# Key scores of a product-key memory laid out key by key instead of head by head, on one Trainium2 core

## The chip, the core and the metric

The kernel runs on one core of a Trainium2 chip. Its engines are TensorE (PE: matmul; PEld: weight load), VectorE (DVE), ScalarE (ACT), GpSimd (POOL) and the DMA queues, here all issued by SyncE (SP). The metric is device time in microseconds for one execution of the whole program. An SBUF tensor has 128 partitions; "elements" below are the fp32 values of one partition, and a step is the distance between neighbours in the order in which an instruction goes through them.

## The reference, cut to what matters

The program is a two-layer decoder over 8192 tokens of width 128: attention, cross attention and a memory layer, then attention, cross attention and a mixture of experts. The change lies in the memory layer, a product-key memory with 8 heads and 2 x 32 keys for each head:

```
q = (xn @ w_q.T).reshape(b, n, 2, h, kd).transpose(2, 0, 1, 3, 4)
sim = jnp.einsum('pbnhd,hkpd->pbnhk', q, keys)
s, i = jax.lax.top_k(sim, k)
all_scores = (sx[..., :, None] + sy[..., None, :]).reshape(b, n, h, k * k)
scores, pk = jax.lax.top_k(all_scores, k)
o = jnp.einsum('bnd,bnhkd->bnhk', inputs, w_down)
o = jax.nn.gelu(o, approximate=False) * jax.nn.softmax(scores, axis=-1)
return jnp.einsum('bnhk,bnhkd->bnd', o, w_up)
```

For each token and head: 32 scores on each of two sides, the 8 best of each side, the 8 best of their 64 sums, and a softmax over those 8 that weighs 8 of 1024 experts.

## The kernel before, in words

A tile is 128 tokens, one in each partition; there are 64 tiles. The memory stage runs all of them through a software pipeline: `staggered` takes, for each engine, a list of (lag, step), and in each round an engine runs its steps in the written order, a step of lag l on the tile l rounds back. Two rounds are one turn of the hardware loop. Each engine works through its list strictly in order; semaphores tie the engines together.

What happens to a tile, with the lines of the profile:

- ACT `normed` L857, then PE `key_scores` L1246: one matmul of the tile against `Mk`, 512 columns = 2 sides x 8 heads x 32 keys, into PSUM bank 0. `Mk` is written once at the start of the program (ACT, L696).
- DVE `top_keys` L1773: 16 MAX8 of 32 scores each, one per side and head, give the 8 best (`V8`). DVE `less_best` L1782: all 512 scores less the best of their side and head, into `DIFF`. DVE `best_less` L1791: the same for the 8 best.
- ACT `key_exps` L864, L865: exp of both, into `EX`; the keys' exps go between other terms there, at a step of 5 x 8 floats. ACT `best_one_hot` L878: one-hot of the best key.
- POOL `candidates` L616, L619: products of the best exps. POOL `terms` L630 to L641: four terms for each key and head, written into `EX` and `hots`. POOL `second_one_hot` L646.
- DVE `top_pairs` L1800 (8 MAX8), `pair_floors` L1807, `pair_sums` L1812, `pair_shares` L1817: the 8th best pair of each head, and one over the sum.
- ACT `above_floor` L897: 8 instructions, one per head, write into PSUM (`psABOVE`) where a term is above the floor. DVE `chosen` L1824: the minimum of that and the term, into `sides`. ACT `scaled_one_hots` L887: 8 instructions, one per head, write the one-hots times the share into `sides`.
- DVE `turn_sides` L1832, L1833: transposes in blocks of 32. PE `spread_heads` L1263: 256 small matmuls make the weights of the 1024 experts, in PSUM banks 0 and 1. DVE `turn_back` L1839 transposes them, PE `turn_weights` L1271 turns them again.
- PE `hidden` L1251 and ACT `hidden` L903 (gelu): the token against all 1024 experts. DVE `gated` L1845: product of both. PE `mixed` L1277: times the experts' outputs. DVE `add_memory` L1849 adds it to the token, `stats_with_memory` L1854 takes its statistics.

PSUM bank 0 holds the scores of one tile and then half of the expert weights of an earlier one. So `spread_heads` of a tile waits until `less_best` of the tile four rounds later has read its scores:

```
pe.wait_ge(d_ready, T.ahead(4, 0, NT))
```

The order on each engine is written out by hand:

```
staggered(nc, pe, NT, [(6, mixed), (0, key_scores), (4, hidden), (5, turn_weights), (4, spread_heads)])
staggered(nc, dve, NT, [(2, top_pairs), (0, top_keys), (2, pair_floors), (2, pair_sums), (7, stats_with_memory), (0, less_best), (3, chosen), (5, gated),
                        (3, turn_sides), (4, turn_back), (5, add_memory), (2, pair_shares), (0, best_less)])
staggered(nc, act, NT, [(0, normed), (2, exps_before_gelu), (5, hidden), (2, exps_after_gelu), (2, best_one_hot), (3, above_floor),
                        (3, scaled_one_hots)])
staggered(nc, pool, NT, [(0, candidates), (1, second_one_hot), (0, terms)])
```

The exps come before the gelu in every second round and after it in the others, so that ACT loads one table set in a round.

Before the change the scores of a tile lie as side, head, key, with the key innermost. `DIFF` and `hots` lie in the same order; `EX` and `sides` lie key by key, with the head innermost.

Of the kernel before, what the change touches and what calls it, by code (L numbers as in the profile page):

```python
# [7 lines left out]
P = 128  # L8
# [11 lines left out]
NKEY = 32  # L20
BLOCK = 32
PH = 8
# [13 lines left out]
ALU = mybir.AluOpType  # L36
ACT = mybir.ActivationFunctionType
# [39 lines left out]
def need(eng, sem, value):  # L77

    if isinstance(value, int) and value <= 0:
        return  # L80
    eng.wait_ge(sem, value)
# [26 lines left out]
def build(nc, x, ctxT, ctx, mask, consts, rows, cols, wq0, wk0, wv0, wo0, xWq, xWk, xWvT, xWeT, wqk, keysT, key_inT,  # L108
# [3 lines left out]
    with ExitStack() as es:  # L112
        def sb(name, shape, dt=F32):
            return es.enter_context(nc.sbuf_tensor(name, shape, dt))

        def sem(name):
            return es.enter_context(nc.semaphore(name))
# [13 lines left out]
        Mk = sb("Mk", [P, 2 * PH * NKEY])  # L131
# [20 lines left out]
        def C(name):  # L152
            a, n = CONST[name]
            return cst[:, a:a + n]
# [24 lines left out]
        top = [0]  # L179

        def carve(n):
            a = top[0]
            top[0] += n
            assert top[0] <= WORK, top[0]
            return work[:, a:a + n]
# [53 lines left out]
        NS = PH * NKEY  # L239
        BEST = 2 * PH * TOPK  # L240
# [4 lines left out]
        DIFF = carve(2 * (BEST + 2 * NS)).rearrange("p (u n) -> p u n", u=2)  # L245
        EX = carve(2 * (BEST + 5 * NS)).rearrange("p (u n) -> p u n", u=2)
        V8 = carve(2 * BEST).rearrange("p (u n k) -> p u n k", u=2, k=TOPK)
# [2 lines left out]
        Z = carve(2 * PH).rearrange("p (u h) -> p u h", u=2)  # L250
        FLOOR = carve(2 * PH).rearrange("p (u h) -> p u h", u=2)
        RZ = carve(2 * PH).rearrange("p (u h) -> p u h", u=2)
        hots = carve(4 * 2 * NS).rearrange("p (r s h k) -> p s r h k", r=4, s=2, h=PH)
        IN2 = [hots[:, :, 2 + u] for u in range(2)]
        KI = carve(NEXP)
        sides = carve(8 * NS)
        XY = sides.rearrange("p (k n h) -> p n h k", n=8, h=PH)
        XT = carve(2 * NEXP).rearrange("p (u k t) -> p u k t", u=2, k=NKEY)
        YT = carve(2 * NEXP).rearrange("p (u k t) -> p u k t", u=2, k=NKEY)
        WT = carve(NEXP)  # L260
# [5 lines left out]
            return DIFF[:, u, 0:BEST].rearrange("p (s h k) -> p s h k", s=2, h=PH)  # L266

        def keys_diff(u):
            return DIFF[:, u, BEST:].rearrange("p (s h k) -> p s h k", s=2, h=PH)

        def by_key(u):
            return EX[:, u, BEST:].rearrange("p (k n h) -> p k n h", n=5, h=PH)

        def keys_of(u):
            return by_key(u)[:, :, 0:2].rearrange("p k s h -> p s h k")

        def best_of(u):
            return EX[:, u, 0:BEST].rearrange("p (s h k) -> p s h k", s=2, h=PH)

        def terms_of(u):  # L280
            return by_key(u)[:, :, 1:5]

        WIDE_Y, REST, DEEP_X = 1, 2, 3
        FAR = 2.0 ** 100
        NEXT_BELOW = 1.0 - 2.0 ** -24
        chosen_terms = XY[:, 2:6].rearrange("p n h k -> p k (n h)")
        one_hot_sides = sides.rearrange("p (k a r h) -> p a r h k", a=4, r=2, h=PH)[:, 0:4:3]
        x_side, y_side = [sides.rearrange("p (k a n) -> p k a n", k=NKEY, a=4)[:, :, a:4:2] for a in range(2)]

        def one_hots_of(u):  # L290
            return hots[:, :, u:4:2]
# [46 lines left out]
        ps = es.enter_context(nc.psum_tensor("ps", [P, 8, 512], F32))  # L338

        def bank(b, a, n=P):  # L340
            return ps[:, b, a:a + n]
# [14 lines left out]
        def group_bank(b, n=P):  # L356
# [7 lines left out]
        psTurn, psRoute = group_bank(6), group_bank(6, MOE)  # L364

        psW = ps[:, 0:2, :].rearrange("p q (k t) -> p q k t", k=NKEY)
        psABOVE = ps[:, 2:4, :].rearrange("p q (k n h) -> p (q k) n h", n=4, h=PH)
        psG = ps[:, 4:6, :].rearrange("p b (c d) -> p (b c) d", d=P)
        psH = ps[:, 6:8, :].rearrange("p b (c d) -> p (b c) d", d=P)
        psM = bank(4, 0)  # L370
        psSim = ps[:, 0, :]
# [24 lines left out]
        ones_ready, sums_done, quantised, folds_done, folds_ready, bound_ready = (  # L396
            sem("ones_ready"), sem("sums_done"), sem("quantised"), sem("folds_done"), sem("folds_ready"), sem("bound_ready"))
# [27 lines left out]
        xb_ready, sim_done, v8_ready, d_ready, ex_ready = (  # L425
            sem("xb_ready"), sem("sim_done"), sem("v8_ready"), sem("d_ready"), sem("ex_ready"))
# [98 lines left out]
        def _(pool):  # L525
# [5 lines left out]
            for u in range(2):  # L531
                ins = pool.tensor_copy(VB[:, u, :], C("vones_pairs"))
# [12 lines left out]
            for n, part in enumerate((bias_parts[:, 0], bias_parts[:, 1], bias_rest[:, 1])):  # L545
                to = bias_rest[:, 2] if n == 2 else bias_rest[:, 0] if n == 0 else bias_b[:, :]
                ins = pool.tensor_tensor(to, part, part_rows[:, n:n + 1].to_broadcast([P, P]), ALU.mult)
# [75 lines left out]
            def terms(T):  # L623

                u = T.u
                x, y = keys_of(u)[:, 0], keys_of(u)[:, 1]
                second = best_of(u)[:, :, :, 1:2].to_broadcast([P, 2, PH, NKEY])
                rest, deep, wide = [terms_of(u)[:, :, n].rearrange("p k h -> p h k") for n in (REST, DEEP_X, WIDE_Y)]
                need(pool, scaled_ready, T.before(2))
                pool.tensor_tensor(IN2[u], keys_of(u), second, ALU.subtract).then_inc(less_second, 1)  # L630
                pool.tensor_tensor(wide, y, second[:, 0], ALU.mult)
                pool.wait_ge(less_second, T.now())
                pool.sem_inc(rank_seen, 1)
                pool.tensor_scalar(IN2[u], IN2[u], 0.0, None, ALU.is_ge).then_inc(in2_ready, 1)
                pool.wait_ge(in2_ready, T.now())
                pool.sem_inc(rank_seen, 1)
                pool.tensor_scalar(rest, IN2[u][:, 0], -1.0, 1.0, ALU.mult, ALU.add).then_inc(far_ready, 1)
                pool.wait_ge(far_ready, T.now())
                pool.tensor_tensor(rest, rest, x, ALU.mult).then_inc(rest_ready, 1)
                pool.wait_ge(rest_ready, T.now())  # L640
                pool.tensor_tensor(deep, rest, second[:, 1], ALU.mult).then_inc(terms_ready, 1)  # L641
# [45 lines left out]
        def _(act):  # L687
# [5 lines left out]
            act.activation(small[:, A1, :], bank(0, 0), ACT.Copy)  # L693
            act.activation(small[:, A2, :], bank(0, P), ACT.Copy)
            act.activation(sc[:, 30:31], bank(5, 0, 1), ACT.Copy)
            act.activation(Mk[:, :], ps[:, 1, :], ACT.Copy).then_inc(folds_ready, 1)  # L696

            def deviations(n, width=NT):
                act.wait_ge(var_ready, n)
# [160 lines left out]
            def key_exps(T):  # L860
                need(act, xy_ready, T.before(2))
                act.wait_ge(d_ready, T.now())
                act.wait_ge(best_less_ready, T.now())
                act.activation(EX[:, T.u, 0:BEST], DIFF[:, T.u, 0:BEST], ACT.Exp)  # L864
                act.activation(keys_of(T.u), keys_diff(T.u), ACT.Exp).then_inc(ex_ready, 1)  # L865

            def exps_before_gelu(T):
                if T.u == 1:
                    key_exps(T)
# [5 lines left out]
            def best_one_hot(T):  # L875
                act.wait_ge(d_ready, T.now())
                need(act, scaled_ready, T.before(2))
                act.activation(hots[:, :, T.u], keys_diff(T.u), ACT.Relu, scale=FAR, bias=1.0).then_inc(top_ready, 1)  # L878

            def scaled_one_hots(T):  # L880

                u = T.u
                act.wait_ge(hot_ready, T.now())
                act.wait_ge(rz_ready, T.now())
                need(act, sides_ready, T.before(1))
                for h in range(PH):
                    ins = act.activation(one_hot_sides[:, :, :, h, :], one_hots_of(u)[:, :, :, h, :], ACT.Copy, scale=RZ[:, u, h:h + 1])  # L887
                ins.then_inc(scaled_ready, 1)

            def above_floor(T):  # L890
# [28 lines left out]
            for e in range(0, MOE, 2):  # L919
                ins = act.activation(d_up[:, e:e + 2].rearrange("p e c d -> p (e c d)"),  # L920
                                     down_w[:, e:e + 2].rearrange("p e c d -> p (e c d)"), ACT.Copy)
# [494 lines left out]
        def _(dve):  # L1416
# [345 lines left out]
            dve.sem_inc(phase, 1)  # L1762


            sim = psSim.rearrange("p (n k) -> p n k", k=NKEY)

            def top_keys(T):

                need(dve, best_less_ready, T.before(2))
                dve.wait_ge(sim_done, T.now())  # L1770
                dve.sem_inc(sim_seen, 1)
                for n in range(2 * PH):
                    ins = dve.max(V8[:, T.u, n, :], sim[:, n, :])  # L1773
                ins.then_inc(v8_ready, 1)

            def less_best(T):

                u = T.u
                top = V8[:, u].rearrange("p (s h) k -> p s h k", s=2)[:, :, :, 0:1]
                dve.wait_ge(v8_ready, T.now())  # L1780
                need(dve, top_ready, T.before(2))
                dve.tensor_tensor(keys_diff(u), sim.rearrange("p (s h) k -> p s h k", s=2), top.to_broadcast([P, 2, PH, NKEY]),  # L1782
                                  ALU.subtract).then_inc(d_ready, 1)

            def best_less(T):
# [33 lines left out]
            def chosen(T):  # L1819

                u = T.u
                dve.wait_ge(share_ready, T.now())
                need(dve, sides_ready, T.before(1))
                dve.tensor_tensor(chosen_terms, psABOVE.rearrange("p k n h -> p k (n h)"), terms_of(u).rearrange("p k n h -> p k (n h)"), ALU.min)\  # L1824
                    .then_inc(xy_ready, 1)

            def turn_sides(T):
# [296 lines left out]
```

## Time and profile before

| | |
|---|---|
| time, median of 3 runs | 2624.07 us (2623.74 to 2628.8) |
| the profiled execution's own time | 2623.28 us |
| its span, first to last instruction | 2621.5 us |
| mean granted TensorE clock | 0.945 of full |
| memory stage, first to last L1263 | 611.6 to 1300.7 us |
| busy over the whole span | PE 89%, DVE 78%, ACT 76%, POOL 35% |

The span is one execution as the hardware profiler saw it. "Busy" is the time in which an engine had an instruction under way; instructions of one engine overlap a little at their ends, so the sum of durations is larger than the time they fill. What an instruction costs the next one is better read from the distance between starts. A wait is the idle time of an engine before an instruction, put down to what released it.

### The profile page before, as it was taken

How to read it: one execution, taken by the hardware profiler on the slowest of the kernel's cores; microseconds unless marked ns; L12 is line 12 of the kernel's file. 1: busy time of each engine (PE TensorE's matmuls, PEld its weight loads, DVE VectorE, ACT ScalarE, POOL GpSimd, SP SyncE). 2: the span in 40 equal slices, each digit the busy share in tenths (PEclk: the TensorE clock that was granted, in tenths of full speed). 3: DMA queues.
4: the chain of work that ended last, by engine and by line, in shares of the span. 5: the costliest groups of instructions: out<-in, count | busy, mean ns of one | idle time of the engine just before them, and what ended most of it. 6: DMA issues, size and time to landing. Idle time of an engine off the chain costs nothing.

```text
span 2621.5 us, 95503 instructions
## 1 busy us (share of the span) xinstructions
PE 2336.3 (89%) x34892; PEld 1856.8 (71%) x34892; DVE 2032.4 (78%) x5455; ACT 1987.0 (76%) x3656; POOL 926.1 (35%) x1203
## 2 busy tenths in 40 slices
PE   2999943966888899988889999899899999999999
PEld 1676733645888888888857767566688788888887
DVE  6788889667799999999667777688766777777776
ACT  1888852778799999999667777788567777777776
POOL 1555510337677777777433333233100000000000
PEclk9999975987799999999899999899799999999999
DMA  5000000000000000000020000111111111111111
GB/s 183 1 0 0 0 17 0 1 0 3 1 0 0 0 0 0 0 0 0 3 66 0 0 0 0 35 44 43 30 43 45 49 57 52 57 51 54 52 57 45
DMA packets 56808, 64.82 MB, mean 25 GB/s; under 512 B 7696, under 2 KB 35088, under 8 KB 56592
## 3 DMA queue, kind: packets, MB, share of 16 engines
q1 hardware_dynamic: 56720, 63.65, 8.0%
q8 instruction: 54, 0.88, 0.1%
q14 instruction: 34, 0.28, 0.0%
HBM read 59.17 MB, written 4.46 MB: 24 GB/s over the span
## 4 chain that ended last, share of the span: by engine, by line
PE 78%; DVE 9%; issue 6%; ACT 4%; SPq 1%; POOL 1%; DVEq 1%; ACTq 0%; POOLq 0%; DMA 0%
PE ps L1263 9%; PE ps L1121 5%; PE ps L1078 5%; PE ps L1106 5%; PE ps L1277 5%; PE ps L1351 4%; PE ps L1373 4%; PE ps L1375 4%; PE ps L1374 4%; PE ps L1353 4%; PE ps L1352 4%; PE ps L1134 3%; PE ps L1093 3%; PE ps L1165 2%; PE ps L1029 2%
## 5 line engine op out<-in xcount | busy, mean ns | idle before, releaser
L562 POOL TENSOR_TENSOR work<-work,consts_sb 128x1024 f32<-128x1024 f32 x128 | 245.9, 1921 | 389.5 <-ACT work L729 346.8
L1263 PE MATMUL ps<-work 32*32 32x32 f32 x16384 | 249.4, 225 | 74.4 <-DVE work L1782 60.2
L1263 PEld LDWEIGHTS ps<-work 32*32 32x32 f32 x16384 | 242.1, 145 | 88.8 <-issue 88.8
L1991 DVE TENSOR_TENSOR h_low<-consts_sb,h_up 128x1024 fp32r<-128x1024 f32 x128 | 156.7, 1224 | 116.3 <-ACT h_up L967 116.3
L1589 DVE TENSOR_REDUCE work<-ps 128x8 f32<-128x512 f32 x256 | 169.8, 686 | 84.8 <-PE ps L1078 79.0
L897 ACT ACTIVATE ps<-work 128x128 f32<-128x128 f32 x512 | 216.6, 478 | 4.0 <-POOL work L641 3.3
L1351 PE MATMUL ps<-a_low,w_up 128*128 128x512 f32 x512 | 205.9, 402 | 0.0
L1373 PE MATMUL ps<-h_low,d_up 128*128 128x512 f32 x512 | 199.9, 390 | 2.2 <-DVE h_low L1991 2.2
L1353 PE MATMUL ps<-a_up,w_low 128*128 128x512 f32 x512 | 200.7, 392 | 0.0
L1352 PE MATMUL ps<-a_up,w_up 128*128 128x512 f32 x512 | 200.4, 391 | 0.0
L1375 PE MATMUL ps<-h_up,d_low 128*128 128x512 f32 x512 | 199.5, 390 | 0.0
L1374 PE MATMUL ps<-h_up,d_up 128*128 128x512 f32 x512 | 199.3, 389 | 0.0
L1991 DVE TENSOR_TENSOR h_low<-small_w,h_up 128x1024 fp32r<-128x1024 f32 x128 | 156.8, 1225 | 52.9 <-ACT h_up L967 52.9
L887 ACT ACTIVATE work<-work 128x128 f32<-128x128 f32 x512 | 163.9, 497 | 17.2 <-issue 17.1
L960 ACT ACTIVATE consts_sb<-ps 128x1024 f32<-128x1024 f32 x128 | 131.8, 1029 | 57.6 <-PE ps L1353 54.3
L967 ACT ACTIVATE h_up<-consts_sb 128x1024 fp32r<-128x1024 f32 x128 | 135.8, 1061 | 49.7 <-PE ps L1375 49.6
L967 ACT ACTIVATE h_up<-small_w 128x1024 fp32r<-128x1024 f32 x128 | 135.8, 1061 | 49.6 <-PE ps L1375 49.5
L1599 DVE TENSOR_TENSOR work<-ps,work 128x512 f32<-128x512 f32 x256 | 169.0, 681 | 0.0
L1106 PE MATMUL ps<-consts_sb,work 128*128 128x128 f32 x1024 | 160.7, 280 | 0.3 <-ACT work L712 0.2
L748 ACT ACTIVATE work<-ps 64x128 f32<-64x128 f32 x256 | 72.2, 282 | 114.0 <-PE ps L1059 77.4
L960 ACT ACTIVATE small_w<-ps 128x1024 f32<-128x1024 f32 x128 | 131.5, 1027 | 34.8 <-PE ps L1353 34.8
L1277 PE MATMUL ps<-w 128*128 128x128 f32 x1024 | 149.2, 306 | 3.5 <-DVE w L1845 1.4
(298 smaller groups left out, 6338.9 us busy)
## 6 DMA issues: line engine op xcount, KB each, us to landing
gates_spread<-gate_rows SPq DMA_DIRECT2D x128, 256.0 KB, 3.1
ctxT_all<-in_ctxT SPq DMA_DIRECT2D x1, 4096.0 KB, 12.7
work<-in_ctx SPq DMA_DIRECT2D x64, 64.0 KB, 1.8
work<-in_ctxT SPq DMA_DIRECT2D x64, 64.0 KB, 1.8
out<-x_all SPq DMA_DIRECT2D x16, 256.0 KB, 3.5
big<-in_up SPq DMA_DIRECT2D x1, 2048.0 KB, 8.7
consts_sb<-in_consts SPq DMA_DIRECT2D x1, 936.0 KB
w<-in_key_inT SPq DMA_DIRECT2D x1, 512.0 KB, 3.7
```

The lines of the kernel that those rows point to most:

```text
L960: act.activation(hid[n], psU[n], ACT.Gelu_apprx_tanh).then_inc(hid_ready, 1)
L967: act.activation(h_up[:, n], hid[n], ACT.Copy).then_inc(h_up_ready, 1)
L1106: ins = pe.transpose(psPT[:, half, n * P:n * P + P], PQ[:, T.u, i * P:i * P + P], ident)
L1263: ins = pe.matmul(psW[rows, n // 16, :, n % 16], XT[rows, T.u, :, n], YT[rows, T.u, :, n], start=True, stop=True)
L1277: ins = pe.matmul(psM, HG[:, c, :], kout[:, c, :], start=c == 0, stop=c == CHUNKS - 1)
L1351: pe.matmul(to, upper, a_low[:, u, :], start=True, stop=False)
L1352: pe.matmul(to, upper, a_up[:, u, :], start=False, stop=False)
L1353: ins = pe.matmul(to, lower, a_up[:, u, :], start=False, stop=True)
L1373: pe.matmul(psD[e % 2], d_up[:, e, at, :], h_low[:, k % RING, c, :], start=first and c == 0, stop=False)
L1374: pe.matmul(psD[e % 2], d_up[:, e, at, :], h_up[:, k % RING, c, :], start=False, stop=False)
L1375: ins = pe.matmul(psD[e % 2], d_low[:, e, at, :], h_up[:, k % RING, c, :], start=False, stop=last and c == 1)
L1991: dve.tensor_tensor(h_low[:, n], hid[n], h_up[:, n].bitcast(F32), ALU.subtract).then_inc(h_split, 1)
```

## The change

The columns of `Mk` are written in another order, so that the scores leave PE as side, key, head, with the head innermost. `DIFF`, `hots` and `psABOVE` follow, and in `EX` the keys' exps stand in one piece behind the best ones'. `sides` stays as it was. With that:

- L1773 reads its 32 scores at a step of 8 floats instead of in a line;
- L1782 reads the best scores at a step of 8 floats over the inner 8 heads, instead of one value over the inner 32;
- L864 and L865 become one instruction of 640 elements, all in a line;
- L878, L646 stay in a line; POOL's `terms` read and write in a line, but for the second best score;
- L887 reads its 32 keys at a step of 8 floats instead of in a line, and writes as before;
- L897 reads at steps of 8 floats throughout (before: 8 and 40) and writes as before;
- L1824 reads in a line, and writes runs of 8 floats instead of 32;
- L696 writes `Mk` at a step of 8 floats.

```diff
--- before.py
+++ after.py
@@ -250,11 +250,11 @@
         Z = carve(2 * PH).rearrange("p (u h) -> p u h", u=2)
         FLOOR = carve(2 * PH).rearrange("p (u h) -> p u h", u=2)
         RZ = carve(2 * PH).rearrange("p (u h) -> p u h", u=2)
-        hots = carve(4 * 2 * NS).rearrange("p (r s h k) -> p s r h k", r=4, s=2, h=PH)
+        hots = carve(4 * 2 * NS).rearrange("p (r s k h) -> p s r k h", r=4, s=2, h=PH)
         IN2 = [hots[:, :, 2 + u] for u in range(2)]
         KI = carve(NEXP)
         sides = carve(8 * NS)
-        XY = sides.rearrange("p (k n h) -> p n h k", n=8, h=PH)
+        XY = sides.rearrange("p (k n h) -> p n k h", n=8, h=PH)
         XT = carve(2 * NEXP).rearrange("p (u k t) -> p u k t", u=2, k=NKEY)
         YT = carve(2 * NEXP).rearrange("p (u k t) -> p u k t", u=2, k=NKEY)
         WT = carve(NEXP)
@@ -266,25 +266,22 @@
             return DIFF[:, u, 0:BEST].rearrange("p (s h k) -> p s h k", s=2, h=PH)
 
         def keys_diff(u):
-            return DIFF[:, u, BEST:].rearrange("p (s h k) -> p s h k", s=2, h=PH)
-
-        def by_key(u):
-            return EX[:, u, BEST:].rearrange("p (k n h) -> p k n h", n=5, h=PH)
+            return DIFF[:, u, BEST:].rearrange("p (s k h) -> p s k h", s=2, h=PH)
 
         def keys_of(u):
-            return by_key(u)[:, :, 0:2].rearrange("p k s h -> p s h k")
+            return EX[:, u, BEST:BEST + 2 * NS].rearrange("p (s k h) -> p s k h", s=2, h=PH)
 
         def best_of(u):
             return EX[:, u, 0:BEST].rearrange("p (s h k) -> p s h k", s=2, h=PH)
 
         def terms_of(u):
-            return by_key(u)[:, :, 1:5]
+            return EX[:, u, BEST + NS:BEST + 5 * NS].rearrange("p (n k h) -> p n k h", n=4, h=PH)
 
         WIDE_Y, REST, DEEP_X = 1, 2, 3
         FAR = 2.0 ** 100
         NEXT_BELOW = 1.0 - 2.0 ** -24
-        chosen_terms = XY[:, 2:6].rearrange("p n h k -> p k (n h)")
-        one_hot_sides = sides.rearrange("p (k a r h) -> p a r h k", a=4, r=2, h=PH)[:, 0:4:3]
+        chosen_terms = XY[:, 2:6]
+        one_hot_sides = sides.rearrange("p (k a r h) -> p a r k h", a=4, r=2, h=PH)[:, 0:4:3]
         x_side, y_side = [sides.rearrange("p (k a n) -> p k a n", k=NKEY, a=4)[:, :, a:4:2] for a in range(2)]
 
         def one_hots_of(u):
@@ -364,7 +361,7 @@
         psTurn, psRoute = group_bank(6), group_bank(6, MOE)
 
         psW = ps[:, 0:2, :].rearrange("p q (k t) -> p q k t", k=NKEY)
-        psABOVE = ps[:, 2:4, :].rearrange("p q (k n h) -> p (q k) n h", n=4, h=PH)
+        psABOVE = ps[:, 2:4, :].rearrange("p q (n k h) -> p (q n) k h", n=2, h=PH)
         psG = ps[:, 4:6, :].rearrange("p b (c d) -> p (b c) d", d=P)
         psH = ps[:, 6:8, :].rearrange("p b (c d) -> p (b c) d", d=P)
         psM = bank(4, 0)
@@ -624,8 +621,8 @@
 
                 u = T.u
                 x, y = keys_of(u)[:, 0], keys_of(u)[:, 1]
-                second = best_of(u)[:, :, :, 1:2].to_broadcast([P, 2, PH, NKEY])
-                rest, deep, wide = [terms_of(u)[:, :, n].rearrange("p k h -> p h k") for n in (REST, DEEP_X, WIDE_Y)]
+                second = best_of(u)[:, :, :, 1].unsqueeze(2).to_broadcast([P, 2, NKEY, PH])
+                rest, deep, wide = [terms_of(u)[:, n] for n in (REST, DEEP_X, WIDE_Y)]
                 need(pool, scaled_ready, T.before(2))
                 pool.tensor_tensor(IN2[u], keys_of(u), second, ALU.subtract).then_inc(less_second, 1)
                 pool.tensor_tensor(wide, y, second[:, 0], ALU.mult)
@@ -693,7 +690,7 @@
             act.activation(small[:, A1, :], bank(0, 0), ACT.Copy)
             act.activation(small[:, A2, :], bank(0, P), ACT.Copy)
             act.activation(sc[:, 30:31], bank(5, 0, 1), ACT.Copy)
-            act.activation(Mk[:, :], ps[:, 1, :], ACT.Copy).then_inc(folds_ready, 1)
+            act.activation(Mk[:, :].rearrange("p (s k h) -> p s h k", s=2, h=PH), ps[:, 1, :].rearrange("p (s h k) -> p s h k", s=2, h=PH), ACT.Copy).then_inc(folds_ready, 1)
 
             def deviations(n, width=NT):
                 act.wait_ge(var_ready, n)
@@ -861,8 +858,7 @@
                 need(act, xy_ready, T.before(2))
                 act.wait_ge(d_ready, T.now())
                 act.wait_ge(best_less_ready, T.now())
-                act.activation(EX[:, T.u, 0:BEST], DIFF[:, T.u, 0:BEST], ACT.Exp)
-                act.activation(keys_of(T.u), keys_diff(T.u), ACT.Exp).then_inc(ex_ready, 1)
+                act.activation(EX[:, T.u, 0:BEST + 2 * NS], DIFF[:, T.u], ACT.Exp).then_inc(ex_ready, 1)
 
             def exps_before_gelu(T):
                 if T.u == 1:
@@ -884,7 +880,7 @@
                 act.wait_ge(rz_ready, T.now())
                 need(act, sides_ready, T.before(1))
                 for h in range(PH):
-                    ins = act.activation(one_hot_sides[:, :, :, h, :], one_hots_of(u)[:, :, :, h, :], ACT.Copy, scale=RZ[:, u, h:h + 1])
+                    ins = act.activation(one_hot_sides[:, :, :, :, h], one_hots_of(u)[:, :, :, :, h], ACT.Copy, scale=RZ[:, u, h:h + 1])
                 ins.then_inc(scaled_ready, 1)
 
             def above_floor(T):
@@ -1762,7 +1758,7 @@
             dve.sem_inc(phase, 1)
 
 
-            sim = psSim.rearrange("p (n k) -> p n k", k=NKEY)
+            sim = psSim.rearrange("p (s k h) -> p s k h", s=2, h=PH)
 
             def top_keys(T):
 
@@ -1770,16 +1766,16 @@
                 dve.wait_ge(sim_done, T.now())
                 dve.sem_inc(sim_seen, 1)
                 for n in range(2 * PH):
-                    ins = dve.max(V8[:, T.u, n, :], sim[:, n, :])
+                    ins = dve.max(V8[:, T.u, n, :], sim[:, n // PH, :, n % PH])
                 ins.then_inc(v8_ready, 1)
 
             def less_best(T):
 
                 u = T.u
-                top = V8[:, u].rearrange("p (s h) k -> p s h k", s=2)[:, :, :, 0:1]
+                top = V8[:, u].rearrange("p (s h) k -> p s h k", s=2)[:, :, :, 0].unsqueeze(2)
                 dve.wait_ge(v8_ready, T.now())
                 need(dve, top_ready, T.before(2))
-                dve.tensor_tensor(keys_diff(u), sim.rearrange("p (s h) k -> p s h k", s=2), top.to_broadcast([P, 2, PH, NKEY]),
+                dve.tensor_tensor(keys_diff(u), sim, top.to_broadcast([P, 2, NKEY, PH]),
                                   ALU.subtract).then_inc(d_ready, 1)
 
             def best_less(T):
@@ -1821,7 +1817,7 @@
                 u = T.u
                 dve.wait_ge(share_ready, T.now())
                 need(dve, sides_ready, T.before(1))
-                dve.tensor_tensor(chosen_terms, psABOVE.rearrange("p k n h -> p k (n h)"), terms_of(u).rearrange("p k n h -> p k (n h)"), ALU.min)\
+                dve.tensor_tensor(chosen_terms, psABOVE, terms_of(u), ALU.min)\
                     .then_inc(xy_ready, 1)
 
             def turn_sides(T):
```

## Rows read from the trace of the kernel before

**Rows 1.** Waits, 700 to 1240 us: engine, line, releaser: total us, times, longest.
```profile
POOL work L616 <- ACT work L865: 105.6, 33, 4.0
...
PE ps L1263 <- DVE work L1782: 54.2, 51, 1.7
DVE x_all L1849 <- PE ps L1277: 37.3, 51, 1.7
...
ACT work L864 <- DVE work L1824: 20.0, 25, 1.9
```

**Rows 2.** Timeline of DVE, 900 to 924 us: start us, duration us, instruction.
```profile
901.67 0.29 DVE L1849 TENSOR_TENSOR x_all<-ps,x_all 128x128 f32 x1 [0.69 <-PE ps L1277]
...
903.35 1.65 DVE L1773 MAX8 work<-ps 128x8 f32<-128x32 f32 x16
904.92 0.15 DVE L1807 TENSOR_SCALAR work<-work 128x8 f32<-128x8 f32 x1
...
905.32 0.67 DVE L1782 TENSOR_TENSOR work<-ps,work 128x512 f32<-128x512 f32 x1
...
912.20 0.29 DVE L1849 TENSOR_TENSOR x_all<-ps,x_all 128x128 f32 x1 [0.55 <-PE ps L1277]
```

**Rows 3.** Timeline of PE, 900 to 924 us.
```profile
906.22 3.85 PE L1263 MATMUL ps<-work 32*32 32x32 f32 x256 [1.18 <-DVE work L1782]
910.00 2.05 PE L1277 MATMUL ps<-w 128*128 128x128 f32 x16
```

**Rows 4.** Line L1263: PE's idle time before it, us and times.
```profile
  DVE work L1782: 60.2, 59
```

**Rows 5.** DVE's lines, 700 to 1240 us: instruction, shapes, count, busy us, mean ns.
```profile
L1773 DVE MAX8 work<-ps 128x8 f32<-128x32 f32 x816 | 83.8, 176 | 0.0
...
L1839 DVE STREAM_TRANSPOSE work<-ps 128x1024 f32<-128x1024 f32 x51 | 61.1, 1199 | 0.0
...
L1807 DVE TENSOR_SCALAR work<-work 128x8 f32<-128x8 f32 x51 | 10.6, 207 | 0.0
```

**Rows 6.** L1506 over the span (ns min/median/max), and DVE's timeline near 53 us.
```profile
L1506 DVE TENSOR_TENSOR t<-st_all x6: 261/262/265, 50.9 to 1858.1; 128x64 f32<-128x64 f32 x6
...
53.46 0.22 DVE L1520 TENSOR_TENSOR t<-t,mv 128x64 f32<-128x64 f32 x1
```

**Rows 7.** ACT's lines, 700 to 1240 us.
```profile
L865 ACT ACTIVATE work<-work 128x512 f32<-128x512 f32 x51 | 61.3, 1202 | 0.0
...
L878 ACT ACTIVATE work<-work 128x512 f32<-128x512 f32 x51 | 32.4, 635 | 0.0
```

**Rows 8.** DVE's lines in other stages, 880 to 1700 us.
```profile
L1619 DVE TENSOR_TENSOR work<-ps,work 128x128 f32<-128x128 f32 x64 | 18.5, 290 | 0.1
...
L1900 DVE TENSOR_TENSOR work<-ps,work 128x128 f32<-128x128 f32 x13 | 3.8, 291 | 1.2
```

**Rows 9.** Timeline of ACT, 900 to 924 us.
```profile
907.15 0.31 ACT L864 ACTIVATE work<-work 128x128 f32<-128x128 f32 x1 [0.35 <-DVE work L1824]
...
908.63 1.28 ACT L903 ACT_TABLE_LOAD   x1
...
910.84 0.62 ACT L878 ACTIVATE work<-work 128x512 f32<-128x512 f32 x1
911.36 3.40 ACT L897 ACTIVATE ps<-work 128x128 f32<-128x128 f32 x8
914.69 2.56 ACT L887 ACTIVATE work<-work 128x128 f32<-128x128 f32 x8
...
919.74 0.31 ACT L864 ACTIVATE work<-work 128x128 f32<-128x128 f32 x1
...
920.92 0.64 ACT L878 ACTIVATE work<-work 128x512 f32<-128x512 f32 x1
```

**Rows 10.** POOL's lines, 700 to 1240 us.
```profile
L646 POOL TENSOR_TENSOR work<-work 128x512 f32<-128x512 f32 x51 | 65.2, 1279 | 0.0
L639 POOL TENSOR_TENSOR work<-work 128x256 f32<-128x256 f32 x51 | 64.0, 1254 | 4.2
```

## The prediction

> **What bounds the kernel now.** The diff touches one stage, so I went first to the waits and the timelines inside it. The stage works on 64 tiles of 128 tokens; between 700 and 1240 us its lines run 51 times (L1839, [rows 5]), so a tile takes 540 / 51 = 10.59 us. All engines are nearly full there, so shares don't tell which sets the 10.59; the waits do [rows 1]. PE waits for DVE's L1782 before L1263 in all 51 tiles, DVE waits for PE's L1277 before L1849 in all 51. These two waits are a ring, and one turn of it can be read off [rows 2, 3]: DVE starts L1849 at 901.67 and runs in order through its two groups of MAX8 (L1800, L1773) to L1782, which starts at 905.32 and lasts 0.67; 0.23 us after its end, at 906.22, PE starts L1263 (3.85 us) and at 910.00 L1277 (2.05 us), which ends at 912.05; at 912.20 DVE starts the next L1849. DVE 4.32, PE 5.83, hand-overs 0.38: 10.53 us. Over the whole stage L1263 was released by L1782 in 59 of 64 tiles [rows 4]; in the others the pipeline fills or PE was late itself.
>
> So an edit to DVE's work between L1849 and L1782 counts at full length, 59 times. DVE's other half (L1824, L1845, three transposes) lies beside PE's 5.8 us and ends 37.3 / 51 = 0.73 us early [rows 1]: that much may be added there free. ACT waits 20.0 us for L1824, so its work is at most (540 - 20.0) / 51 = 10.20 us a tile, 0.39 below the ring. POOL waits 105.6 us, 2.07 us a tile. Nothing that makes ACT or POOL shorter shortens the ring by itself.
>
> **The change part by part.** The matmul of the scores keeps its shape; only its columns come in another order. All the rest are access patterns, and the count of instructions changes in one place (two exps become one). No wait, no DMA and no queue is added or moved.
>
> (a) L1782, less_best, on the ring. 512 elements; the scores come from PSUM in a line as before. The second operand, the best score of each head, is now V8 at a step of 8 floats (32 bytes) over the inner 8 heads, run over again for each of 32 keys; before, it stood still over the inner 32 elements. The nearest rows for what a stepped read costs DVE [rows 6]: L1506 combines two 64-element columns of st_all, each at a step of 24 bytes, and takes 262 ns; L1520, as many elements in a line, 0.22 us. That is 0.04 / 64 = 0.62 ns more an element. L1506 has both operands stepped, L1782 will have one; I take the same 0.62, since an element waits for its later operand and not for the sum: 512 x 0.62 = 0.32 us a tile, 59 x 0.32 = 18.9 us. Lower end nothing (two streams could have been in each other's way in L1506). Upper end by ACT's stepped write [rows 7]: 512 elements at 160 bytes in 1202 ns (L865), in a line in 635 (L878), 1.1 ns each, so 0.57 us a tile, 33 us. I see no reason for a gain.
>
> The Trainium skill, SBUF — State Buffer, Specifications (TRN2), has 16-byte cachelines that want two hits each for full bandwidth, with a penalty for each crossing to a new line. The two pairs of rows above agree with it, and by it (a) is no accident of L1506.
>
> (b) L1773, 16 MAX8 of 32 elements, on the ring. They now read PSUM at a step of 32 bytes. They follow each other at (1.65 - 0.18) / 15 = 98 ns [rows 2, 5]. No row shows DVE reading PSUM at a step element by element; L1839 reads it in runs of 16 floats at 1199 ns for 1024 elements, 1.17 ns each, no sign of a cost. Lower end nothing; upper end that of (a), since 16 x 32 is again 512 elements: 0.32 us a tile by 0.62 ns, 0.57 by 1.1. I take nothing: every slow row is of SBUF, and the nearest of PSUM, L1839, is not slow. It is the weakest step of the sum.
>
> The Trainium skill, Advanced Engine Details and Errata, Memory Cachelines, gives PSUM lines of 8 bytes and asks for every two consecutive elements to be contiguous for best throughput. It speaks of matmuls; if it holds for MAX8 too, it speaks against this change and gives rival B.
>
> (c) L1824, the minimum, beside PE. Its inputs are now in a line, its output in runs of 8 floats instead of 32, one run every 256 bytes. L1900 writes runs of 8 in 291 ns, L1619 as many elements in a line in 290, both from PSUM [rows 8]. Nothing; and 0.73 us of slack would cover 0.7 ns on each of its 1024 elements. With the cover gone, it would count as (a) does.
>
> (d) ACT's exps. L864 (128 elements) and L865 (512, written at 160 bytes) become one of 640 in a line. From the start of L864 to that of what follows L865 it is 1.48 us where a table load follows (907.15 to 908.63) and 1.18 where not (919.74 to 920.92) [rows 9]. L878, 512 in a line, is followed after 0.52 us; 128 elements more are (635 - 310) / 384 x 128 = 108 ns, from L864's 0.31 us: 0.63, and 0.74 of duration before a table load. Saved 0.74 and 0.55 in turn, 0.65 us a tile, off the ring.
>
> (e) ACT's eight L887 keep their stepped write and now read at 32 bytes. L897 has the same count, also one column operand, and reads (and writes, to PSUM) at 32 bytes already. Spacing: L887 (2.56 - 0.50) / 7 = 0.294 us, L897 (3.40 - 0.48) / 7 = 0.417 [rows 9]. I put the 0.123 between them down to the stepped read and take it for L887: 8 x 0.123 = +0.98 us a tile. Lower end nothing (if it is L897's write to PSUM that costs), upper end 0.25, twice, if stepped read and stepped write can't overlap. L897 itself keeps its steps on both sides.
>
> ACT after: 10.20 - 0.65 + 0.98 = 10.53 us a tile, just below the old ring and 0.38 below the new one of 10.91. Hidden.
>
> (f) POOL. L639, 256 elements with all three operands at 160 bytes, takes 1254 ns; L646 takes 1279 for 512 in a line [rows 10]. Half of that is 0.64: -0.6 us. The others lose one step and gain one (the second best score, now stepped inside); bounded by L639's excess, +0.6 us for L630. POOL idles 2.07 us a tile: nothing either way, but for what it may free (rival E).
>
> (g) Once: ACT writes Mk stepped at 46 us, 512 x 1.1 = at most 0.57 us, with DVE then busy until 50. Nothing.
>
> **Sum.** The profiled execution took 2623.28 us (span 2621.5, 1.8 around it), 0.8 below the median of the three runs. 2623.3 + 18.9 = 2642.2, against the median 2643. I say 2643, its own range 2636 (a third of the term lost) to 2657 (upper end of (a)).
>
> **The rivals.** B: MAX8 is slowed as well. For it: nothing in the trace shows such a read at full rate. Against: L1839. 59 x (0.32 + 0.32) = 38 us: 2662; with 0.57 for each 67 us, 2691.
>
> C: ACT becomes the bound. It decides from (10.91 - 9.55) / 8 = 0.17 us more in each L887. At 0.25 ACT's work is 11.55, and 59 x (11.55 - 10.59) = 57 us: 2681. For it: ACT is only 0.39 under the ring. Against: L897, stepped on both sides, is 0.123 over L887.
>
> D: no change. The stepped operand of L1782 comes in time beside the PSUM stream, and MAX8 is as before. The ring stays at 10.59, ACT's 10.53 hides: 2624, from 2619 to 2629. For it: nothing was shown of one stepped operand.
>
> E: faster. As D, and less meeting of DVE and POOL: L1807, 8 elements, takes 207 ns in the mean [rows 5] where 0.15 is enough [rows 2], and stands on the ring; 0.06 x 64 = 4 us. As much again if ACT, let off L865, gives the ring fewer late starts: 8 us, 2616. For it: POOL and ACT each lose 0.6 us a tile. Against: the ring waits for neither by these rows.
>
> **How the numbers follow.** Forecast 0.38, B 0.22, C 0.08, D 0.17, E 0.15. A measurement of this kernel can tell about 0.2% (5.2 us) from no change. Slower by more: 0.38 + 0.22 + 0.08 = 0.68; within: 0.17; faster: 0.15. The range of 8 in 10 starts at 2616 (half of E left out) and ends at 2678 (more than half of C and the upper end of B left out).
>
> **What the profile after would show.** L1782 at about 0.99 us instead of 0.67 if (a) holds; 16 L1773 still in 1.65 us, 2.0 if B; L1263 still 0.23 us behind L1782, at a distance of 10.9 us from the last; L887 spaced 0.41 us; one exp of 0.74 us; L639 near 0.7. If L1782 keeps its 0.67 the forecast's only term is gone, and D or E is left. If PE's and DVE's two waits shrink and both wait for ACT instead, it is C.

## The result, and the profile after

The changed kernel takes 2660.08 us (median of 4 runs, 2655.87 to 2665.75) against 2624.18 us: 1.0134 times as long, 95% interval 1.0112 to 1.0156, so 36 us slower. The profiled execution spans 2658.6 us. The forecast was 2643 in a range of 2616 to 2678: the sign and the range hold, the middle is 17 us low. In the new file the lines of the stage stand 3 or 4 lower: less_best is L1778 (L1782 before), spread_heads L1259 (L1263), best_less L1787 (L1791), add_memory L1845 (L1849), the scaled one-hots L883 (L887).

DVE's timeline after, the same columns and the same stretch as [rows 2]:

```profile
913.92 0.29 DVE L1845 TENSOR_TENSOR x_all<-ps,x_all 128x128 f32 x1 [0.66 <-PE ps L1273]
914.13 0.19 DVE L1813 RECIPROCAL work<-work 128x8 f32<-128x8 f32 x1
914.24 1.18 DVE L1787 TENSOR_TENSOR work<-work 128x128 f32<-128x128 f32 x1
915.34 0.80 DVE L1796 MAX8 work<-work 128x8 f32<-128x28 f32 x8
916.06 1.65 DVE L1769 MAX8 work<-ps 128x8 f32<-128x32 f32 x16
...
918.02 1.05 DVE L1778 TENSOR_TENSOR work<-ps,work 128x512 f32<-128x512 f32 x1
```

Less_best takes 1.05 us instead of 0.67. The 16 MAX8 take 1.65 us, as before: reading PSUM at a step costs them nothing. Best_less, which the change did not touch, takes 1.18 us here; in this stage its shortest is 0.24. POOL's timeline shows what it met:

```profile
913.75 1.52 POOL L627 TENSOR_TENSOR work<-work 128x512 f32<-128x512 f32 x1
915.22 0.91 POOL L628 TENSOR_TENSOR work<-work 128x256 f32<-128x256 f32 x1
```

Both instructions read two SBUF operands; L1787 starts while L627 runs and ends 0.15 us after it. Below, "DVE meets POOL" stands for this. PE's timeline and its granted clock (in the second view, stretches of 2 us with each engine's busy time, the third number from the right, 1.00 being full):

```profile
919.31 3.86 PE L1259 MATMUL ps<-work 32*32 32x32 f32 x256 [2.03 <-DVE work L1778]
923.10 2.66 PE L1273 MATMUL ps<-w 128*128 128x128 f32 x16
```

```profile
918.00:920.00 2.00, 0.69 (x49) 0.72 (x52) 2.00 (x3) 1.38 (x4) 1.80 (x3) 1.00 0.00 0
920.00:922.00 2.00, 2.00 (x156) 2.00 (x152) 2.00 (x3) 1.74 (x2) 0.94 (x3) 0.75 0.00 0
922.00:924.00 2.00, 2.00 (x87) 1.94 (x80) 2.00 (x3) 1.99 (x4) 2.00 (x2) 0.50 0.00 0
924.00:926.00 2.00, 2.00 (x15) 1.79 (x15) 0.83 (x2) 2.00 (x6) 2.00 (x3) 0.90 0.00 0
```

PE waits 2.03 us in this tile (1.18 in [rows 3]; the means are 1.57 and 1.04). Soon after, the granted clock is at 0.50 of full, 1.2 instead of 2.4 GHz, for some 3 us, and L1273's 16 matmuls take 2.66 us instead of 2.05. Counted in stretches of 2 us from 740 to 1240, there are 16 such dips after and 5 before. After, all 11 tiles in which PE had waited over 1.8 us have one, and 5 of the other 34; before, no wait was that long.

The waits after, 735 to 1240 us (45 tiles):

```profile
PE ps L1259 <- DVE work L1778: 70.6, 45, 2.2
DVE x_all L1845 <- PE ps L1273: 39.0, 45, 1.8
ACT work L861 <- DVE work L1820: 26.5, 23, 2.1
```

It is the ring of [rows 1], only longer: PE and DVE still wait for each other once in each tile, and ACT still waits for DVE. From the starts in DVE's and PE's timelines between 735 and 1240 us the tile can be split (mean us of a tile; the column "DVE meets POOL" is the distance from best_less to the next MAX8, "PE's part" from spread_heads to DVE's add_memory):

| kernel | tile | less_best | DVE meets POOL | PE's part | granted clock |
|---|---|---|---|---|---|
| before | 10.57 | 0.67 | 0.47 | 6.16 | 0.98 |
| after | 11.22 | 1.05 | 0.57 | 6.30 | 0.95 |
| difference | +0.65 | +0.39 | +0.10 | +0.14 | |

That is 0.65 x 59 = 38 us, against 36 measured: 23 us less_best itself, 6 best_less held up by POOL, 8 the lower clock, and 0.03 us a tile besides, since L1803 (L1807 before) meets POOL too. That the 0.14 us of PE's part is the clock can be seen tile by tile: in tiles without a dip PE's part is 6.05 us before and 6.06 after, in the 5 that hold one before it is 7.1, in the 16 that hold one after 6.7.

### The profile page after: what moved, and what is told of

Same layout as the page of the kernel before. It is cut to its first block, busy times and chain, and to the rows that moved or that the text cites. A ratio compares the mean times of both kernels' runs of the same rounds, so it can differ in the third digit from the quotient of the medians.

```text
span 2658.6 us, 95439 instructions
## 1 busy us (share of the span) xinstructions
PE 2344.7 (88%) x34892; PEld 1864.2 (70%) x34892; DVE 2063.7 (78%) x5455; ACT 2016.4 (76%) x3592; POOL 897.7 (34%) x1203
## 4 chain that ended last, share of the span: by engine, by line
PE 76%; DVE 11%; issue 6%; ACT 4%; SPq 1%; POOL 1%; DVEq 1%; ACTq 0%; POOLq 0%; DMA 0%
PE ps L1259 9%; PE ps L1074 5%; PE ps L1117 5%; PE ps L1102 5%; PE ps L1273 5%; PE ps L1347 4%; PE ps L1369 4%; PE ps L1349 4%; PE ps L1371 4%; PE ps L1348 4%; PE ps L1370 4%; PE ps L1130 3%; PE ps L1089 3%; DVE work L1769 2%; DVE work L1778 2%
## 5 line engine op out<-in xcount | busy, mean ns | idle before, releaser
L1259 PE MATMUL ps<-work 32*32 32x32 f32 x16384 | 249.5, 226 | 104.3 <-DVE work L1778 89.9
L1259 PEld LDWEIGHTS ps<-work 32*32 32x32 f32 x16384 | 242.0, 145 | 118.7 <-issue 118.6
L883 ACT ACTIVATE work<-work 128x128 f32<-128x128 f32 x512 | 223.1, 526 | 18.7 <-issue 18.7
L1273 PE MATMUL ps<-w 128*128 128x128 f32 x1024 | 156.8, 315 | 3.3 <-DVE w L1841 1.4
```

What stands on the lines that cost most here:

```text
L1259: ins = pe.matmul(psW[rows, n // 16, :, n % 16], XT[rows, T.u, :, n], YT[rows, T.u, :, n], start=True, stop=True)
L1273: ins = pe.matmul(psM, HG[:, c, :], kout[:, c, :], start=c == 0, stop=c == CHUNKS - 1)
```

## The experiments

Two questions: does the step in less_best alone make the 36 us, through the ring, or does ACT? And are the two smaller terms what they seem? Ratios are to the kernel before on the same chip; the runs were made on several chips, so small differences are better read from the ratios than from the medians.

**The step taken away.** `far_best` is a constant tile set up once.

```diff
-                top = V8[:, u].rearrange("p (s h) k -> p s h k", s=2)[:, :, :, 0].unsqueeze(2)
+                top = far_best[:, 0:1].unsqueeze(2).unsqueeze(3)
```

> The changed kernel, but less_best subtracts one constant column (1000, never stepped) instead of the best scores stepped by 32 bytes; the key exps come out as zero, the best ones stay right. Theory 'ring' (what DVE does between add_memory and less_best counts in full): less_best back from 1.05 to 0.67 us, 59 x 0.387 = 22.8 us less than 2660, so 2637; down to 2629 if the dips of the TensorE clock (one in four tiles after, one in ten before) go with it. Rival 'ACT' (its eight stepped reads per tile, +0.98 us, set the pace): the time stays within 5 us of 2660 although less_best is short. Rival 'DVE in sum' agrees with the ring here.

Measured: 1.0064 (1.0039 to 1.0089), median 2637.89 us. Less_best is back:

```profile
L1771 DVE MAX8 work<-ps 128x8 f32<-128x32 f32 x736 | 75.6, 179 | 0.0
...
L1789 DVE TENSOR_TENSOR work<-work 128x128 f32<-128x128 f32 x47 | 38.0, 809 | 0.0
...
L1780 DVE TENSOR_TENSOR work<-ps,far_best 128x512 f32<-128x512 f32 x46 | 30.9, 673 | 0.0
```

As the ring wants, and against ACT, whose stepped reads are all still there. But the rest did not shrink as hoped: there are still 10 dips, and best_less (L1789, 809 ns in the mean, 555 in the changed kernel) is held up by POOL for longer.

**POOL's stepped operand taken away.**

```diff
-                second = best_of(u)[:, :, :, 1].unsqueeze(2).to_broadcast([P, 2, NKEY, PH])
+                second = best_of(u)[:, :, 0:1, 1].unsqueeze(2).to_broadcast([P, 2, NKEY, PH])
```

> The changed kernel, but POOL's terms take the second best of one head per side for all heads, so that this operand stands still instead of stepping by 32 bytes; the terms are wrong. Ring: POOL's first operation of terms falls from 1528 to about 1280 ns, best_less on DVE is blocked by it for less long (the distance from best_less to the next MAX8 goes from 0.57 to 0.47 us in the mean), 59 x 0.1 = 6 us: 2654. Rival (the distance grew because of where POOL starts, not how long it takes): 2660, distance unchanged. ACT: 2660.

> The changed kernel with both edits above. Ring: 22.8 + 6 off, and the PE clock's dips back to about one in ten tiles, 8 us: 2660 - 37 = 2624, 2620 to 2632. If the dips are not due to the longer wait of PE, 2631. ACT: 2660.

Measured: alone 1.0131 (1.0102 to 1.016), both 1.0007 (0.9994 to 1.002). POOL's first operation of terms in the run with both:

```profile
L628 POOL TENSOR_TENSOR work<-work 128x512 f32<-128x512 f32 x47 | 49.9, 1062 | 0.0
```

In the run with this edit alone it falls further than expected, to 1.05 us, which is below the 1.37 it took before the change; the distance to the next MAX8 falls to 0.46 us, as expected. Yet alone this gives about 1 us, less than the intervals can show, since L1803 meets POOL more often instead (its mean goes from 0.22 to 0.26 us). With both edits the whole loss is gone. So the parts don't add: by the ratios 18 and 1 us apart, 33 together. The table below shows why: without the first step but with the second, the distance from best_less to the next MAX8 was 0.73 us a tile, with neither 0.49. One expectation failed: the dips did not go back to one in ten tiles, there are 11 in 47, and PE's part keeps 0.05 of its 0.14 us. And ACT is busy for 502.06 of 505 us in this run, 10.6 us a tile: at a tile of 10.67 it has nothing left to hide in, so with this work on ACT the changed layout had little room to come out faster than before.

**The step alone, in the kernel before.** The cleanest of all: the old layout everywhere, ACT and POOL as they were.

```diff
-                top = V8[:, u].rearrange("p (s h) k -> p s h k", s=2)[:, :, :, 0:1]
+                top = far_best[:, :].rearrange("p (s h k) -> p s h k", s=2, h=PH)[:, :, :, 0].unsqueeze(2)
-                dve.tensor_tensor(keys_diff(u), sim.rearrange("p (s h) k -> p s h k", s=2), top.to_broadcast([P, 2, PH, NKEY]),
+                dve.tensor_tensor(DIFF[:, u, BEST:].rearrange("p (s a b) -> p s a b", s=2, b=PH), psSim.rearrange("p (s a b) -> p s a b", s=2, b=PH), top.to_broadcast([P, 2, NKEY, PH]),
```

> The kernel before, with nothing changed but less_best's second operand, now a constant tile read at a step of 32 bytes over the inner 8 (the key exps come out as zero). Ring: less_best 1.05 us instead of 0.67, 2624 + 22.8 = 2647, and up to 2655 if the longer wait of PE brings clock dips. ACT: 2624, since ACT's reads are as before.

Measured: 1.0143 (1.0119 to 1.0168), 2660.02 us. The step of one operand of one instruction is enough for the whole loss of the change. It is 5 us more than I expected at most: the clock falls more often still (0.94, PE's part 6.34 us, with 19 dips), and L1807 meets POOL (0.34 us instead of 0.18).

**How large a step costs.** The same kernel with other steps, one execution each.

> The kernel before with less_best's second operand, a constant tile, at a step of 8 bytes over the inner 8 (as in the run with the step alone, which had 32). If each change to another piece of 16 bytes costs, this one changes at every second element: less_best 0.67 us, or halfway, 0.86. If any step costs: 1.06.

> The same at a step of 16 bytes: by pieces of 16 bytes less_best takes 1.06 us, as at 32; if the cost begins only at 32 bytes: 0.67.

Less_best at 8, 16 and 32 bytes, in this order:

```profile
L1784 DVE TENSOR_TENSOR work<-ps,far_best 128x512 f32<-128x512 f32 x47 | 31.3, 667 | 0.0
```

```profile
L1784 DVE TENSOR_TENSOR work<-ps,far_best 128x512 f32<-128x512 f32 x45 | 47.6, 1058 | 0.0
```

```profile
L1784 DVE TENSOR_TENSOR work<-ps,far_best 128x512 f32<-128x512 f32 x45 | 47.9, 1065 | 0.0
```

Two elements in each 16 bytes cost nothing; one in each costs (1058 - 667) / 512 = 0.76 ns an element, and a wider step no more. The kernel with 8 bytes took 2628.35 us, the one with 16 took 2662.7. This is what the Trainium skill states in SBUF — State Buffer, Specifications (TRN2): 16-byte cachelines with two hits each for full bandwidth. The size of the cost is from these runs alone.

**ACT's stepped reads taken away.**

```diff
-                    ins = act.activation(one_hot_sides[:, :, :, :, h], one_hots_of(u)[:, :, :, :, h], ACT.Copy, scale=RZ[:, u, h:h + 1])
+                    ins = act.activation(one_hot_sides[:, :, :, :, h], one_hots_of(u).rearrange("p s r k h -> p s r (k h)")[:, :, :, h * NKEY:h * NKEY + NKEY], ACT.Copy, scale=RZ[:, u, h:h + 1])
```

> The changed kernel, but ACT's eight scaled one-hots read 32 keys in a line (values of several heads mixed, wrong) instead of at a step of 32 bytes. Both theories: their spacing falls from 0.42 to 0.29 us, ACT's work by 1.0 us a tile. Ring: the time stays at 2660 within 5, apart from where POOL's operations now meet DVE's (that term has moved by up to 0.3 us a tile, 18 us, between kernels so far). ACT: 2630 or less.

Measured: 1.0141 (1.011 to 1.0172), no gain. ACT now waits for L1820 63.0 us instead of 26.5 in the same stretch:

```profile
ACT work L861 <- DVE work L1820: 63.0, 23, 3.2
```

ACT's reads are dearer, as step (e) said, and pace nothing at this length of the ring. The theory 'ACT' is out.

**The clock by itself.** PE's wait is filled with work that it does twice over.

```diff
-                for c in range(CHUNKS):
+                for c in list(range(CHUNKS)) * 2:
                     ins = pe.transpose(psG[:, c, :], WT[:, c * P:c * P + P], ident)
```

> The changed kernel with turn_weights' eight matmuls done twice over (same result), so that PE works 1.0 us of the 1.3 to 2.0 us that it waits for less_best in each tile; nothing on the ring gets longer. Theory 'clock': the stretches at half clock (one in about four tiles, 0.14 us a tile in PE's part of the ring) come from these waits: the granted clock between 735 and 1240 us goes from 0.95 to 0.98 or more, and the time from 2660 to 2652. Rival: the dips have another cause or come from PE's sum of work: clock 0.95 or lower, 2660 or a little more.

Measured: 1.012 (1.0088 to 1.0153), 2655.96 us. PE before spread_heads waits 37.2 us instead of 70.6, and over the same stretch the clock is full (third number from the right):

```profile
PE ps L1259 <- DVE work L1778: 37.2, 46, 1.2
...
735.00:1240.00 505.00, 466.86 (x14036) 432.27 (x14037) 476.76 (x1626) 483.88 (x954) 352.53 (x410) 1.00 0.00 0
```

One dip is left of 16, and PE's part falls from 6.30 to 6.05 us. So the dips come from PE's waits and not from its work. Of the 0.25 us, DVE gives 0.14 back to POOL (0.71 instead of 0.57). The tile is 0.12 us shorter in the profile, 7 us over the stage; the time shows 4, and as its interval overlaps that of the changed kernel, it would show nothing by itself. What is shown is the clock and PE's part.

**A layout without the steps.** The 8 best of each head are stored rank by rank, so the best scores of the 16 heads lie side by side.

```diff
-        V8 = carve(2 * BEST).rearrange("p (u n k) -> p u n k", u=2, k=TOPK)
+        V8 = carve(2 * BEST).rearrange("p (u k n) -> p u n k", u=2, k=TOPK)
-            return DIFF[:, u, 0:BEST].rearrange("p (s h k) -> p s h k", s=2, h=PH)
+            return DIFF[:, u, 0:BEST].rearrange("p (k n) -> p k n", k=TOPK)
-            return EX[:, u, 0:BEST].rearrange("p (s h k) -> p s h k", s=2, h=PH)
+            return EX[:, u, 0:BEST].rearrange("p (k s h) -> p s h k", s=2, h=PH)
-                best = V8[:, u].rearrange("p (s h) k -> p s h k", s=2)
+                best = V8[:, u].rearrange("p n k -> p k n")
```

> The changed kernel with the 8 best of each head stored rank by rank, so that the best scores of the 16 heads lie side by side: less_best and POOL's terms read them in a line, MAX8 writes its 8 results at a step of 64 bytes, POOL's candidates read at that step. All results are right. Ring: less_best 0.67 us, POOL's first operation of terms 1.28 us, as in the run with both operands still: 2625, 2618 to 2634. If MAX8's stepped writes cost 0.8 ns each: 16 x 8 x 0.8 = 0.1 us a tile, 6 us more. ACT: 2660.

Measured: 1.0013 (0.9996 to 1.003), 2629.07 us.

```profile
L627 POOL TENSOR_TENSOR work<-work 128x512 f32<-128x512 f32 x47 | 61.0, 1298 | 0.0
...
L1778 DVE TENSOR_TENSOR work<-ps,work 128x512 f32<-128x512 f32 x47 | 31.5, 670 | 0.0
```

Less_best is back at 670 ns, POOL's first operation takes 1298, the clock is 0.98. That undoes the loss in a kernel that keeps the rest of the change. It is no faster than before: the shorter exps buy nothing off the ring, and ACT waits for L1820 no more than 3.5 us in 48 tiles, so its dearer reads stand just under the ring.

**The ring cut shorter.** If the ring paces the stage, DVE's order can shorten it.

```diff
-            staggered(nc, dve, NT, [(2, top_pairs), (0, top_keys), (2, pair_floors), ...
-                                    (3, turn_sides), (4, turn_back), (5, add_memory), (2, pair_shares), (0, best_less)])
+            staggered(nc, dve, NT, [(2, top_pairs), (6, add_memory), (0, top_keys), (2, pair_floors), ...
+                                    (3, turn_sides), (4, turn_back), (2, pair_shares), (0, best_less)])
```

> The kernel before with one step of DVE moved: add_memory, which waits for PE's last matmuls of a tile, now stands behind pair_shares, best_less and top_pairs, just ahead of top_keys. Ring: DVE no longer waits 0.73 us with 1.3 us of work at hand; the ring loses those 1.3 us of DVE and gets the matmul of the scores (0.9 us), so it falls from 10.57 to about 9.8 us, below ACT's 10.20, which then sets the pace: 59 x 0.37 = 22 us, 2602, and not under 2600. If ACT or DVE in sum set the pace already: 2624.

> The changed kernel with add_memory moved just ahead of top_keys, as in the run of the kernel before with that move. DVE in sum then sets the pace together with ACT: DVE 10.29 us (that run's tile) + 0.39 for less_best = 10.68, ACT 10.65 (as in the run with both): 2611 + 59 x 0.39 = 2633 at the most, 2626 at least. If the ring still held: 2650.

> Both: best scores rank by rank, and add_memory later. ACT's work is 10.5 us a tile in this layout (its stepped reads, 0.98 us, less the one exp, 0.65), so here ACT should set the pace, where the ring no longer does: 2620, about 18 us slower than the kernel before with the same move. If the stepped reads did not matter at all: 2602 as that one or less.

Measured: in the kernel before 0.9929 (0.9907 to 0.9951), 2609.99 us, faster than both kernels; in the changed kernel 1.0044 (1.0027 to 1.006), 2634.4 us; with the best scores rank by rank 0.9991 (0.9976 to 1.0005), 2623.43 us. The first is 8 us short of what I expected, since best_less, no longer behind the wait, runs into POOL in most tiles:

```profile
L1791 DVE TENSOR_TENSOR work<-work 128x128 f32<-128x128 f32 x49 | 41.4, 846 | 0.0
...
L1807 DVE TENSOR_SCALAR work<-work 128x8 f32<-128x8 f32 x49 | 21.0, 429 | 0.0
```

DVE then has hardly a wait left (3.8 us in 49 tiles), so DVE in sum paces it; ACT, which waits for L1824 5.5 us, is close behind. The third shows where ACT's dearer reads do count: its tile is 10.64 us, ACT waits for nobody, and it is 13 us slower than the first (18 expected). The move makes old and new layout faster. Between them there are still 10.73 - 10.30 = 0.43 us a tile (the second run came 1 us above its expected 2626 to 2633); 0.39 of it is what less_best takes more, and DVE's sum is then the bound, but ACT waits only 5.0 us there, so the runs don't part the two.

All in one table (columns as above, last the ratio):

| kernel | tile | less_best | DVE meets POOL | PE's part | clock | ratio |
|---|---|---|---|---|---|---|
| after | 11.22 | 1.05 | 0.57 | 6.30 | 0.95 | 1.0134 |
| less_best still | 10.89 | 0.67 | 0.73 | 6.21 | 0.96 | 1.0064 |
| POOL's operand still | 11.15 | 1.05 | 0.46 | 6.30 | 0.96 | 1.0131 |
| both still | 10.67 | 0.68 | 0.49 | 6.21 | 0.96 | 1.0007 |
| step alone | 11.25 | 1.06 | 0.48 | 6.34 | 0.94 | 1.0143 |
| one-hots in a line | 11.19 | 1.05 | 0.49 | 6.27 | 0.95 | 1.0141 |
| PE filled | 11.10 | 1.07 | 0.71 | 6.05 | 1.00 | 1.012 |
| best by rank | 10.69 | 0.67 | 0.44 | 6.18 | 0.98 | 1.0013 |

## Why the prediction was right or wrong

**The ring** held in every run: PE waits for less_best and DVE for L1273 in each tile, and what was added to or taken from less_best came out in the time. Counting it 59 times was right (0.65 x 59 = 38 against 36).

**(a)**, the only term of the sum, was the right instruction and mis-sized: 0.32 us a tile forecast, 0.39 measured. 0.76 ns an element is what 16 and 32 bytes cost, against my 0.62. Worth 4 us. About half of it is rounding: I took L1520 as 0.22 us from the timeline, and the trace has 217 ns, so that (262 - 217) / 64 = 0.70 ns and 0.36 us a tile. The other half stays open: L1506 steps by 24 bytes, and no run tried that in less_best.

**What the sum left out** is larger. I let a longer less_best lengthen the ring by itself and no more. It also makes PE wait longer, and a longer wait brings the clock down: 0.14 us a tile, 8 us. The trace of before has a clock of 0.98 in this stretch, which I had not looked up, and I did not ask what made the missing 0.02, nor what a longer wait would do to it. The run with the step alone shows that this is a consequence of (a): there PE's part grows with nothing else changed. The run with PE filled shows that the wait is what does it.

**(f)** said POOL hides. It does, on its own path; but its operations hold up DVE's best_less and L1807, which stand on the ring. I had named that meeting only as a source of gain (rival E). It went the other way by 6 us. POOL's first operation went from 1.37 to 1.53 us, and a longer tile shifts the two against each other; that these two together are the cause is argued, and their shares are not known. How much it costs can't be read from POOL's durations alone: it was 0.44 to 0.73 us a tile in kernels that differ little. That is the least predictable term here.

**(b)** was right at nothing: MAX8 takes 179 ns in the mean, and 16 take 1.65 us. So rival B, whose 2662 is nearest to the result, has the right time by the wrong mechanism, and the PSUM line of 8 bytes in the Trainium skill, Advanced Engine Details and Errata, Memory Cachelines, does not reach a MAX8 of 32 elements at 32 bytes here.

**(c)** was right: the minimum takes 1213 ns with runs of 8, 1206 before. **(d)** and **(e)** were right to 0.01 us: the one exp takes 0.74 us, the one-hots are spaced (3.48 - 0.53) / 7 = 0.42 us:

```profile
911.01 0.74 ACT L861 ACTIVATE work<-work 128x640 f32<-128x640 f32 x1
...
915.52 3.48 ACT L883 ACTIVATE work<-work 128x128 f32<-128x128 f32 x8
```

Rival C needed 0.17 us more in each one-hot and got 0.13. The sum for ACT, 10.53 us a tile, was nearly right too: 10.6 where ACT was full, in the run with both edits. Rivals D and E needed less_best to stay at 0.67; it did not. In **(f)** L639 fell to 0.73 us, 0.7 expected.

**Range.** It held the result by the room left for B and C, not by knowledge of the clock and the meetings with POOL.

## What to carry to other kernels

When a layout is turned so that one operand gains, look at each other operand of the same instructions: what stood still over the inner axis may now step. Before counting on a gain, find the ring of waits that sets the pace; here all savings lay off it and the one loss on it. And cost a longer wait of PE twice, once for itself and once for the clock it brings down.

## What the runs showed of the hardware

- DVE, a second operand from SBUF beside one from PSUM, 512 elements: 667 ns at a step of 8 bytes or in place, 1058 at 16 bytes, 1065 at 32. That even one stepped operand of two costs in full I had only assumed.
- DVE's MAX8 of 32 elements from PSUM at 32 bytes costs nothing (175 to 182 ns, in a line 176 to 182). Writing its 8 results at a step of 64 bytes makes the record 186 ns long, but the 16 still take 1.57 us from the first to what follows them, as in all the runs.
- POOL, 512 elements with two operands, both in SBUF: 1298 ns both in a line, 1528 with the second at 32 bytes, and 1045 to 1062 where it stands still.
- ACT's eight copies, reading at 32 bytes as well as writing at 256: 0.42 us apart, instead of 0.29 where they only write at a step.
- DVE's subtraction of 128 elements with both operands in SBUF: 0.24 us at the shortest, up to 1.19 us where it starts while POOL runs L627 (after).
- TensorE's clock: 16 dips to 1.2 GHz in 500 us with waits of 1.57 us in the mean (up to 2.2), 5 with 1.04, 1 with 0.81, at more work in sum. The mean alone does not tell: with both edits it was 1.09 us, with waits of up to 1.8, and there were 11 dips.
